# A four-layer graph network on one core: node tables stored from 128 partitions, indices held in SBUF, POOL's program written out

## What is computed

```python
# 1 GAT, 4 heads, with a GRU: softmax over incoming edges of leaky(el[src] + er[dst])
msg = feat[src] * alpha[:, :, None];  agg = segment_sum(msg, dst)
# 2 two Chebyshev steps, then GATv2
agg = segment_sum((x * Dinv[:, None])[src], dst)
e = leaky_relu(fsrc[src] + fdst[dst]);  out = segment_sum(fsrc[src] * a, dst)
# 3 spline convolution on a 4 x 4 grid of tents over edge_attr
msg = sum_k basis[:, k:k+1] * (x[edge_index[1]] @ w2[k]);  out = segment_sum(msg, edge_index[0])
# 4 AGNN: softmax of beta * cos(x[dst], x[src])
out = segment_sum(w[:, None] * x[src], dst)
```

## Time and profile before

| what | value |
|---|---|
| median of three runs | 2799.86 us (2793.5 to 2805.55) |
| profiled execution, its time | 2798.72 us |
| its span (first to last instruction) | 2797.0 us |
| POOL busy | 1915.2 us (68%), 1825 instructions |
| PE busy | 1938.7 us (69%) |
| DVE busy | 1784.3 us (64%) |
| ACT busy | 879.6 us (31%) |
| transfers issued by SP | 137.86 MB, 13.3% of 16 engines |
| transfers issued by POOL | 54.88 MB, 12.6% of 16 engines |

### The profile page before, as it was taken

One profiled execution on the slowest core, in us unless ns is written; L12 is line 12 of the kernel. 1 busy time (PEld: TensorE's weight loads), 2 busy tenths in 40 slices (PEclk: granted clock), 3 DMA queues, 4 the chain that ended last, 5 costly groups with the idle time before them and its releaser, 6 DMA issues.

```text
span 2797.0 us, 52360 instructions
## 1 busy us (share of the span) xinstructions
PE 1938.7 (69%) x19915; PEld 1682.9 (60%) x19915; DVE 1784.3 (64%) x4803; ACT 879.6 (31%) x804; POOL 1915.2 (68%) x1825
## 2 busy tenths in 40 slices
PE   2577773669990999643988633487877788359990
PEld 2577773469990999633988611354544455259990
DVE  7499996155551455426878740477777777488785
ACT  0376774134440455310544322000000000125442
POOL 6788883357774777657888630588888887547873
PEclk6789886579995999856999855799999999679995
DMA  6243342123221322113222113211211111323321
GB/s 218 51 130 106 104 130 81 26 53 73 66 61 32 64 66 67 47 34 121 62 61 61 41 55 135 67 46 46 47 46 46 47 46 42 128 49 65 72 55 26
DMA packets 104646, 194.01 MB, mean 69 GB/s; under 512 B 52441, under 2 KB 71713, under 8 KB 100983
## 3 DMA queue, kind: packets, MB, share of 16 engines
q1 hardware_dynamic: 51528, 137.86, 13.3%
q0 software_dynamic: 53024, 54.88, 12.6%
HBM read 107.45 MB, written 85.19 MB: 69 GB/s over the span
## 4 chain that ended last, share of the span: by engine, by line
POOL 26%; issue 13%; DVE 10%; PE 10%; DMA 8%; ACT 1%; POOLq 0%; DVEq 0%; SPq 0%
POOL edges_d L600 16%; PE ps L740 8%; POOL rows L600 7%; DVE edges_d L1302 2%; DMA tab_y_dram<-edges_d 2%; POOL starts_dram L603 1%; POOL agg L600 1%; DMA idx<-cell_dram 1%; POOL fence L686 1%; DMA edges_d<-starts_dram 1%; DMA rows<-tab_fsrc_dram,idx 1%; PE ps L879 1%; DMA rows<-tab_x_dram,idx 1%; DVE bigT L1388 0%; DVE rows L1125 0%
## 5 line engine op out<-in xcount | busy, mean ns | idle before, releaser
L600 POOL DMA_INDIRECT edges_d<-tab_y_dram,idx x425 | 451.6, 1063 | 230.3 <-DMA idx<-cell_dram 113.6
L740 PE MATMUL ps<-nodes,edges_d 125*128 125x160 bf16 x7140 | 499.9, 234 | 101.9 <-ACT edges_d L921 98.4
L740 PEld LDWEIGHTS ps<-nodes,edges_d 125*128 125x128 bf16 x7140 | 498.4, 98 | 103.4 <-ACT edges_d L921 101.0
L785 PE MATMUL ps<-edges_d,scan 125*125 125x480 bf16 x1700 | 388.7, 390 | 142.2 <-DVE edges_d L1718 142.2
L600 POOL DMA_INDIRECT rows<-tab_cheb_dram,idx x374 | 407.0, 1088 | 109.1 <-issue 106.8
L740 PE MATMUL ps<-nodes,aggn 125*128 125x180 bf16 (+2 forms) x3372 | 377.9, 245 | 145.1 <-DVE rows L1125 145.1
L740 PE MATMUL ps<-nodes,agg 125*128 125x180 bf16 (+2 forms) x3564 | 342.6, 246 | 145.6 <-ACT aggn L921 80.7
L785 PEld LDWEIGHTS ps<-edges_d,scan 125*125 125x125 bf16 x1700 | 241.7, 145 | 289.7 <-DVE edges_d L1718 113.9
L1125 DVE COPY_PREDICATED rows<-picks,ps 125x192 f32<-125x192 uint16 (+4 forms) x850 | 342.7, 404 | 75.9 <-PE ps L740 23.3
L740 PEld LDWEIGHTS ps<-nodes,agg 125*128 125x128 bf16 x3564 | 290.1, 102 | 150.3 <-ACT aggn L921 81.4
L740 PEld LDWEIGHTS ps<-nodes,aggn 125*128 125x128 bf16 x3372 | 280.7, 102 | 149.5 <-issue 105.4
(11 more groups left out here) (330 smaller groups left out, 3123.9 us busy)
## 6 DMA issues: line engine op xcount, KB each, us to landing
src<-srcT_dram SPq DMA_DIRECT2D x68, 427.2 KB
scan_dram<-scan SPq DMA_DIRECT2D x17, 1700.0 KB
scan_dram<-scan SPq DMA_DIRECT2D x34, 425.0 KB
tab_y_dram<-edges_d SPq DMA_DIRECT2D x5, 2812.5 KB
scanD_dram<-scan SPq DMA_DIRECT2D x34, 400.0 KB
edges_d<-starts_dram SPq DMA_DIRECT2D x2, 3408.0 KB, 20.1
starts_dram<-scan SPq DMA_DIRECT2D x2, 3400.0 KB, 15.3
edges_d<-tab_y_dram,idx POOLq DMA_INDIRECT x425, 2.6
```

What stands on the lines that cost most here:

```text
L600: pool.indirect_dma_start(o, None, table, bass.IndirectOffsetOnAxis(index, 0)).then_inc(s, SLOT)
L740: ins = pe.matmul(columns_ps[:, i, 0:PICKS * w], hots_[b][lot][:, i * NP:i * NP + P], parts_[:, part, at:at + PICKS * w], start=(lot == 0 ...
L785: ins = pe.matmul(ps[0:NP, lot, 0:PICKS * 3 * D], lot_hots[c][:, t, lot, :], picked[c][:, t, :, :].rearrange("p k c -> p (k c)"), start=(b ...
```

## The change

Four things are edited. Tables and the lots of products are stored from all 128 partitions in place of 125, the broadcast of `src16` goes to 128, and the DRAM tables get P * J rows (128 x 25). The sources are loaded once, as `src_i`, and stay in SBUF, so `idx`, its loads, `idx_in` and SP's wait on `rows_in` go; the cells stay in SBUF too, in what was `attr`, and `cell_dram` goes with its store and loads. The fences go. POOL's loops over chunks and slots are written out as straight code, with constant counts; the other engines keep their loops. Three memsets on 32 partitions and one more load of the sources are new.

```diff
@@ tables
-        tab_y_dram = dram("tab_y_dram", (N * CELLS * CELLS, CORNERS * D))
-        cell_dram = dram("cell_dram", (E,), I32)
+        tab_y_dram = dram("tab_y_dram", (P * J * CELLS * CELLS, CORNERS * D))
-        idx = sb("idx", [P, 2, L], I32)
+        src_i = sb("src_i", [P, T], I32)
-        attr = sb("attr", [NP, T, 2])
+        attr = sb("attr", [P, T, 2])
+        cell_i = attr[:, :, :].rearrange("p t d -> p (t d)")[:, 0:T].bitcast(I32)
-        staged = edges_d[0:NP, 0:2 * LS * YROW].rearrange("p (b j c) -> p b j c", b=2, j=LS)
+        staged = edges_d[:, 0:2 * LS * YROW].rearrange("p (b j c) -> p b j c", b=2, j=LS)
@@ SP
+                    if a is lambda_max_row:
+                        sp.wait_ge(tails_cleared, 1)
+                        sp.dma_start(src_i[0:NP, :], src_grid).then_inc(src_loaded, SLOT)
...
-                        sp.dma_start(src16[0:NP, b, 0:n * NP], srcT_dram[bass.ds(t0 + L - n, n), :]
-                                     .rearrange("t p -> (t p)").partition_broadcast(NP)).then_inc(src16_in[b], SLOT)
+                        sp.dma_start(src16[:, b, 0:n * NP], srcT_dram[bass.ds(t0 + L - n, n), :]
+                                     .rearrange("t p -> (t p)").partition_broadcast(P)).then_inc(src16_in[b], SLOT)
 
                     def step(k, b, t0):
-                        if gathered[b].n or k >= 2:
-                            sp.wait_ge(rows_in[b], gathered[b].at())
-                        sp.dma_start(idx[0:NP, b, :], src_grid[:, bass.ds(t0, L)]).then_inc(idx_in[b], SLOT)
-                        gathered[b].up(SLOT * (L - PE_COLS[name]))
...
-                store_table(tab_cheb_dram[0], tabf[0:NP, 0:J * D])
+                store_table(tab_cheb_dram[0], tabf[:, 0:J * D])
...
-                    if g == 0:
-                        sp.wait_ge(cells_made, 1)
-                        sp.dma_start(cell_grid, cell_i).then_inc(cells_stored, SLOT)
-                sp.wait_ge(cells_stored, SLOT)
...
@@ POOL, run_pass
-                    def step(k, b, t0):
-                        pool.wait_ge(idx_in[b], loaded[b].up(SLOT))
+                    for k in range(CH):
                         if k >= 2:
                             pool.wait_ge(rows_used, used.up())
-
-                        if fences.n:
-                            pool.wait_ge(fence_done, fences.at())
-                        pool.tensor_tensor(fence[:, b:b + 1], ones[:, 0:1], ones[:, 1:2], ALU.add)\
-                            .then_inc(fence_done, 1)
-                        fences.up()
                         for t in range(L - PE_COLS[name]):
-                            gather(rows[:, b, t * width:(t + 1) * width], table, idx[:, b, t:t + 1], rows_in[b])
-
-                    chunks(pool, [(loaded[0], SLOT), (loaded[1], SLOT), (used, 2), (fences, 2)], step)
+                            gather(rows[:, k % 2, t * width:(t + 1) * width], table,
+                                   src_i[:, k * L + t:k * L + t + 1], rows_in[k % 2])
@@ POOL, spline
+                pool.wait_ge(cells_made, 1)
+                for n in range(CH * SLOTS):
+                    if n >= SLOTS:
+                        pool.wait_ge(slot_used, n - SLOTS + 1)
                     for t in range(LS):
-                        gather(slots[:, c, t * CORNERS * D:(t + 1) * CORNERS * D], tab_y_dram,
-                               idx[:, 0, c * LS + t:c * LS + t + 1], slot_in[c])
+                        gather(slots[:, n % SLOTS, t * CORNERS * D:(t + 1) * CORNERS * D], tab_y_dram,
+                               cell_i[:, n * LS + t:n * LS + t + 1], slot_in[n % SLOTS])
@@ DVE, start
+                vec.memset(src_i[96:P, :].bitcast(F32), 0.0)
+                vec.memset(attr[96:P, :, :], 0.0).then_inc(tails_cleared, 1)
+                vec.memset(tab[96:P, :, :], 0.0)
                 vec.memset(rows[0:NP, :, :], 0.0)
```

More of the change, by code:

```diff
@@ L154, in gnn_kernel @@
         dst_i = sb("dst_i", [NP, T], I32)
-        fence = sb("fence", [P, 2])
         same = sb("same", [NP, T])
@@ L289, in gnn_kernel @@
         slot_in = [sem(f"slot_in{c}") for c in range(SLOTS)]
-        slot_idx_in = [sem(f"slot_idx_in{c}") for c in range(SLOTS)]
         slot_used = sem("slot_used")
@@ L528, in _ @@
                         .then_inc(products_stored[g % 2], SLOT)
-                    if g == 0:
-                        sp.wait_ge(cells_made, 1)
-                        sp.dma_start(cell_grid, cell_i).then_inc(cells_stored, SLOT)
-                sp.wait_ge(cells_stored, SLOT)
-                def load_indices(turn0, first):
-                    for c in range(SLOTS):
-                        if not first:
-                            sp.wait_ge(slot_in[c], slot_n[c].up(SLOT * LS))
-                        sp.dma_start(idx[0:NP, 0, c * LS:(c + 1) * LS], cell_grid[:, bass.ds(turn0 + c * LS, LS)])\
-                            .then_inc(slot_idx_in[c], SLOT)
-                slot_n = [Count() for c in range(SLOTS)]
-                load_indices(0, True)
-                with sp.Fori(0, CH - 1) as turn:
-                    for c in slot_n:
-                        c.enter(turn, SLOT * LS)
-                    load_indices(turn * L + L, False)
-                store_table(tab_x3_dram, tabf[0:NP, 0:J * HG])
-                store_table(tab_xn_dram, scatf[0:NP, :])
+                store_table(tab_x3_dram, tabf[:, 0:J * HG])
+                store_table(tab_xn_dram, scatf[:, :])
                 run_pass("agnn", lambda: load_edges(starts32_dram, D, 3 * J + 4))
@@ L650, in _ @@
                 scatter_starts(starts4_dram, H)
+                pool.wait_ge(src_loaded, SLOT)
                 run_pass("gat")
```

75 lines of the change are left out of this document (23 added, 52 removed).

## The result

The changed kernel takes 2667.0 us (median of four runs, 2660.2 to 2675.54) beside 2800.41 us for the kernel before (median of four, same chip): a ratio of 0.953, interval 0.949 to 0.956. That is 133 us less, where 87 were forecast and the range ended at 2686. The profiled execution is the slowest of the four (2675.54, span 2673.4), so a comparison of the two profiled spans shows 123.6 of the 133 us.

The account below looks back on a forecast made before the run. It took the limit to move by stage: the store while products are made, POOL in the sum over edges, DVE, PE or POOL in passes. Savings of 57 + 14 + 12 + 4 - 0.5 = 86.5 us gave 2713 us, range 2686 to 2750.

Parts of the forecast that it names:

- What bounds the kernel: Limit moves by stage: the store while products are made, POOL in the sum over edges at 7.1 us a slot.
- Change 1: Products' stage: storing lots from 128 partitions leaves the making of tiles as the limit; 57 us saved, ends 36 and 63.
- Change 2: Sum over edges: removing its eighty fences saves 14 us, ends 6 and 22.
- POOL is stretched less: Rival in `gatv2` and the sum over edges: a new phase against DVE halves gather stretch, another 50 us, 2663; chance 0.08.
- Change 3: Starts of `cheb0` and `cheb1`: faster table store and broadcast save 6 us each, 12 us together, ends 6 and 14.
- Change 4: The five passes: removing their 85 fences saves 4 us, ends 0 and 15.
- What is added: Straight code, three memsets and a new load of the sources: 0.5 us lost; earlier broadcasts outside the starts give 0.
- The written-out program: Rival on POOL's straight code: instructions fetched too slowly, 2821 us if each gather comes 0.1 us later; slower had chance 0.04.

Follow-up runs that it names:

- split_pick: The changed kernel with DVE's longest two-input operation of a slot (the 1200-element selection) split into 480 and 720 elements; 2705.2 us.
- small_125: The changed kernel with node tables and broadcasts back at 125 partitions, the products' table still at 128; 2689.1 us, ratio 0.962.
- fence_first: The changed kernel with one fence back ahead of the first gather of each of 80 slots of the sum over edges; 2706.2 us, ratio 0.967.
- stores_only: The kernel before with only storage, tables and broadcasts over 128 partitions; index loads, fences and loops stay; 2717.4 us, ratio 0.972.
- train_late: The changed kernel with the first of a slot's five DVE comparisons moved ahead of its first two-input multiplication; 2666.6 us.
- one_input: The changed kernel with DVE's seven two-input operations of each slot in the sum over edges made one-input, their values left out; 2635.3 us.

## Why the prediction came out as it did

- **What bounds the kernel.** Right for the products' stage and for the sum over edges.
- **Change 1, 57 us: right, 62.5 measured.** The step mis-sized is the store's rate. It was priced at the loads' 365 GB/s and 11.5 us to land; it runs at 442 GB/s and lands in 8.2 us. Lots follow at 10.7 us and not 11.0, and ACT never waits for a store, only for PE (14.7 us in 20 waits). The making of the tiles is the limit, as predicted.
- **Change 2, 14 us with ends 6 and 22: wrong, 41.** This is the step that failed. It took the fences' busy time and asked only whether the hold on the long fence would go or pass to the gather behind it. It took the gathers' own stretch (44 us in this stage, by its count) as fixed. The runs showed that stretch to depend on the phase: 20 of the 41 us are gathers that are no longer held. Before, in one slot of two, a gather was held by 0.4 us at the multiplication and another by 0.3 us at L1716, 17.8 and 13.5 us in all; these holds fell to 1.8 and 0.9, while those at L1703 and L1718 (L1651 and L1666 in the changed kernel) grew from 18.2 to 28.4. The case stood among the rivals as "POOL is stretched less", with 0.08 and about the right size (half of 44 us in this stage). What was held against it, that DVE's work is tied to the gathers' landing, is just what makes one place of the pattern repeat from slot to slot. That the changed kernel fell on the good side of the step at the multiplication is luck: nothing in the prediction could tell it, and split_pick, shifted by some 0.1 us, is 33 us slower. The other half of that rival, in `gatv2`, did not come: 2 us.
- **Change 3, 12 us: right, 6.8 + 4.7 with the passes behind.** POOL's first gathers come 9.3 and 8.5 us sooner after the aggregation, but the passes, in which TensorE is the limit, take POOL 2.3 and 3.6 us longer. DVE's wait for the broadcast in `cheb1` fell from 7.13 us to 1.38.
- **Change 4, 4 us: too small.** The measured price of the passes' fences is 12 us between medians. The traces place some 4 of it in `agnn` and 2.4 in the sum over edges (563.6 beside 561.2); where the rest lies stays open.
- **What is added, -0.5 us: wrong in sign, +4.1.** The memsets cost nothing that shows. The claim that failed is that broadcasts outside the starts give 0. In the preparation, DVE's wait for the rows gathered by destination fell from 4.96 us to 0.53, as the changed kernel's timeline shows:

```profile
37.56 0.34 SPq L441 DMA_DIRECT2D tab_dram<-tab  x1
37.95 1.49 SPq L473 DMA_DIRECT2D src<-srcT_dram  x2
...
51.22 0.66 DVE L1209 TENSOR_SCALAR_CACHE_REDUCE edges_d<-edges_d,node_f 125x425 f32<-125x425 int32 x1 [0.53 <-DMA edges_d<-in_dst,row_of]
```

  It was not a wait for POOL, whose gathers stand where they stood. The table and the broadcasts were in flight with them, and small_125, with 125 partitions for just those, has the loss back. That they crowd a few DMA engines is argued from this, not shown by a trace.
- **The written-out program:** no loss. The gaps stay at 0.30, and fence_first, without loops, has the stage length of stores_only, which has them.

By steps the forecast had 87 and the profiled spans 124: 5.5 of the difference are the store, 27 the fences of the sum over edges, 4.6 the preparation. The 10 us between the spans' gain and the medians' lie within the spread of the changed kernel's own executions (2660 to 2676); in the profiled one `gatv2` takes 338 us, where six of the ten kernels without pass fences have 330 to 333. What makes it the one or the other stays open.

No version tried here beats the changed kernel with all of the computation in it: train_late's 2666.6 us is the same time. one_input's 2635 us shows what is left to win from the holds, some 30 us.

## What to carry to other kernels

Where POOL issues gathers in a loop and DVE's work starts on their landing, the two repeat one pattern: take the gathers' extra time over their shortest, match it with the DVE operation in which they start, and price a change of POOL's program between none and all of that stretch, not by the instructions that it adds or removes. Changes of 0.1 to 0.4 us a slot in either program made the stage 10 to 40 us longer in four kernels, and 3 us shorter in a fifth. And look first at the DMA share inside a slow store: 0.31 against 1.03 for 125 against 128 partitions was worth half of the whole gain.

## What was not expected of the hardware

- The hold has a sharp edge: a gather that starts 0.00 to 0.04 us after DVE's two-input 125x640 multiplication takes 0.94 us (91 of 91), one at 0.06 to 0.12 us takes 1.5 to 1.6 (57 of 57). At the operation L1716 the edge lies ahead of its recorded start: gathers that began 0.12 us before it were held (43 of 43 in the kernel before).
- A gather in flight does not keep a two-input operation of DVE waiting: 410 multiplications that began 0.06 to 0.60 us into a gather lasted 0.81 to 0.83 us.
- The gather's end follows the end of the holding operation by 0.81 us (0.94 - 0.13), whichever operation it is.
- A 1.40 us DVE operation with one bfloat16 input never held a gather (0 of 168); a 0.49 us one with one float32 input held every gather that began inside it 0.045 us or later (44 of 44), and none that began sooner (0 of 23).
- A store from 128 partitions ran at 442 GB/s, faster than the 365 GB/s of the loads in the earlier trace rows.
